# Row-maximum scores of two heads in separate halves of the partitions, and softmax denominators passed on by transfers, in a causal attention

## The chip, the cores and the metric

One Trainium2 chip, one core. The time is device time in microseconds of one execution of the whole program, the median of the runs; the profile is of one further execution.

## The reference

Two pre-norm layers on `x` of shape (4, 1024, 128), each an attention and a mixture of experts with residuals. The change touches the first attention only:

```python
def _L0_attn_ref(x, Wq, bq, Wk, bk, Wv, bv, Wo, bo):     # 16 heads of 8
    q, k, v = split_heads(x @ Wq + bq), split_heads(x @ Wk + bk), split_heads(x @ Wv + bv)
    scores = jnp.einsum('bhqd,bhkd->bhqk', q, k) / jnp.sqrt(8)
    scores = jnp.where(causal, scores, -10000.0)
    probs = jax.nn.softmax(scores, axis=-1)
    ctx = jnp.einsum('bhqk,bhkd->bhqd', probs, v)
    return ctx.transpose(0, 2, 1, 3).reshape(B, S, 128) @ Wo + bo
...
x = x + _L0_attn_ref(_layernorm(x, axis=-1), ...)
```

## The kernel before

`project` writes q and k to DRAM as three bf16 parts each (`q_parts`, `k_parts`). `attention0` walks 16 iterations `it`, each of one batch element and G = 4 heads, in 48 slots `p`. A product of q and k is the sum of the nine products of parts, so the operands `qs` and `ks` hold 9 x 8 = 72 partitions (STACK) for a head, and there are two kinds of scores.

- Scores for the maximum: queries on the partitions, `S`, a ring of three PSUM banks. The list `A` has 48 pieces for one iteration: query blocks 7 to 0, up to 512 keys each, four heads for each piece. PE multiplies, DVE reduces a piece to its maximum (`mx`). These run ahead (`AHEAD`, 72 slots): slots 0 to 23 of `it` make pieces 24 to 47 of iteration `it+1`, slots 24 to 47 pieces 0 to 23 of `it+2`. So the operands of `it+2` must be there at slot 24. They lie in one of three thirds of `qs` and `ks` (`half`).
- Transposed scores for the exponent: keys on the partitions, `ST`, two banks. Three further rows, STACK to STACK+2, hold minus the maximum in three parts against rows of ones, so the product comes out with the maximum subtracted. PE makes one piece a slot (`GROUPS`), ACT applies `Exp` into `eT`.

Every fourth slot PE multiplies `eT` of four heads by `vx` into `O`, four heads in four strips of 32 PSUM columns; row 8 of each strip gets the sum of the exponents. DVE copies `O` to `num` at slots 20 (`COPY0`, first half of the queries) and 4 of the next iteration (`COPY1`). PE multiplies `num` by `den_row`, which puts each head's sum on the rows of its strip (`extra`), DVE takes the reciprocal in eight pieces of 64 columns, one a slot from `RDEN0` = 36 and `RDEN1` = 10, and POOL multiplies (`normalize`) into `ctxT`.

The maximum: when `mx` is complete DVE makes `top` at slot 24, PE turns it to 32 x 128 in `extra` at slot 26, DVE splits it in `parts` (slots 27 to 30), and SP copies the three parts to the rows of `qs` (`store_max`).

SP issues all transfers, in the order of `step(it)`: `load(it+2)` (18) once the scores of slot 0 are made, `load_v(it+1)`, `store_max(it+1)` (3), `pack(it-1)` (4, to `packed`). PE waits for `max_in` at slot 0 and for `kq_in` before the first piece of an iteration. PE and DVE run a loop over iterations 1 to 13 with register offsets; the rest is written out. SP is written out in full.

Of the kernel before, what the change touches and what calls it, by code (L numbers as in the profile page):

```python
# [6 lines left out]
ALU = mybir.AluOpType  # L7
ACT = mybir.ActivationFunctionType
AX = mybir.AxisListType.X
# [5 lines left out]
P = 128  # L15
# [58 lines left out]
def build(nc, inp, out):  # L74
    k = Core()
    with ExitStack() as ctx:
        def sb(name, shape, dt=F32):
# [6 lines left out]
                    nc.dram_tensor("v_ones", (TOK, H * (HD + 1)), F32, kind="Internal").ap()]  # L84
        k.route_w = nc.dram_tensor("route_w", (B, 2), F32, kind="Internal").ap()
# [403 lines left out]
def attention0(nc, k, ctxT, packed):  # L489
# [18 lines left out]
    with ExitStack() as ctx:  # L508
# [3 lines left out]
        def sb(name, shape, dt=F32):  # L512
# [15 lines left out]
        score_s, max_s, top_s, turn_s, part_s = sem("score"), sem("max"), sem("top"), sem("turn"), sem("part")  # L528
        sturn_s, e_done, pv, oc, den_s, rden_s, ctx_s, vx_s = (
            sem(x) for x in ("sturn", "exp", "pv", "o_copied", "den", "rden", "ctx", "vx"))  # L530
# [42 lines left out]
        COPY0, DEN0, RDEN0 = G * FIRST_HALF + 4, G * FIRST_HALF + 18, G * FIRST_HALF + 20  # L573
        COPY1, DEN1, RDEN1 = 4, 8, 10
        RSTEPS = 8

        @block.sync
        def _(sp):
            def load(x):
                for u in range(SPLIT):  # L580
                    for y in range(SPLIT):
                        rows = slice((u * SPLIT + y) * HD, (u * SPLIT + y + 1) * HD)
                        for dst, src, s in ((qs, k.q_parts, u), (ks, k.k_parts, y)):
                            sp.dma_start(dst[rows, bass.ds(half(x), G * SEQ)].rearrange("d (g t) -> d g t", g=G),
                                         src[s, bass.ds(x * G * HD, G * HD), :].rearrange("(g d) t -> d g t", d=HD)).then_inc(kq_in, 16)
# [32 lines left out]

            sp.wait_ge(kones_s, 1)
            load(0)  # L620
            load_v(0)
            sp.wait_ge(kq_in, 16 * 2 * TERMS)
            load(1)
            store_max(0)
            for it in range(ITERS):
                step(it)
            pack(ITERS - 1)
            sp.wait_ge(packed_s, 16 * G * ITERS)
            sp.wait_ge(max_in, 16 * SPLIT * ITERS)
# [3 lines left out]
        def _(pe):  # L633
            def slot(it, p):
                x, r, na = max_piece(it, p)
                if x is not None:
                    i, j, lo, hi = A[r]
# [10 lines left out]
                if live(it):  # L648
                    hf, kb, lo, hi = GROUPS[p // G]
                    j = p % G  # L650
                    if p == 0:
                        pe.wait_ge(max_in, 16 * SPLIT * (it + 1))
# [1377 lines left out]
```

## Time and profile before

| | us |
|---|---|
| median of 3 runs | 4088.49 (4086.24 to 4089.66) |
| profiled execution, own time | 4076.11 |
| its span | 4074.2 |
| first attention, first issue of its loads to the product after it | 116.6 to 833.6 |
| DVE, PE, ACT busy in the whole span | 2963.6, 2823.3, 2477.3 |

Busy times are from records of single instructions; those of PE overlap, so a busy PE is not PE at its peak. PEclk is the granted clock of PE, 1.00 for 2.4 GHz and 0.50 for 1.2 GHz. An `x3` behind a row says that three like it were merged. In brackets stands how long the engine had been idle, and what released it.

### The profile page before, as it was taken

What the parts mean: (1) busy time and instruction counts of PE and PEld (TensorE: products, weight loads), DVE (VectorE), ACT (ScalarE), POOL (GpSimd) and SP (SyncE); (2) the same over time, 40 slices, a digit from 0 to 9 for tenths busy, and PEclk for the clock granted to TensorE, in tenths of its full rate; (3) what the DMA queues carried; (4) which work ended last, traced back from release to release, by engine and by line L of the source; (5) the groups of instructions that cost most, each with busy time, mean ns of one, the idle gap of its engine ahead of it and who ended that gap; (6) DMA issues with size and microseconds to landing.
All of it is one profiled execution on the core that took longest, in us unless ns stands there. A gap on an engine that the chain in (4) does not pass through costs nothing. (4 is left out here: it accounts for less than half of the span.)

```text
span 4074.2 us, 92993 instructions
## 1 busy us (share of the span) xinstructions
PE 2823.3 (69%) x25270; PEld 1692.7 (42%) x25318; DVE 2963.6 (73%) x10992; ACT 2477.3 (61%) x4212; POOL 1793.1 (44%) x4286
## 2 busy tenths in 40 slices
PE   3688888849554666656565666666666666665999
PEld 2133333336342444434343444444444444444665
DVE  6677777531454888888787888888888888864444
ACT  2155555624312888867686887888888888862222
POOL 3000000020013777756575776777776767653000
PEclk9699999959765666766666776776776776676999
DMA  3222232100012000001000001000001000000000
GB/s 111 39 36 35 33 39 30 19 8 26 10 50 72 5 4 7 4 4 36 4 4 4 7 4 36 4 7 4 4 13 27 7 4 5 6 1 27 6 8 8
DMA packets 131770, 77.04 MB, mean 19 GB/s; under 512 B 73287, under 2 KB 116055, under 8 KB 131463
## 3 DMA queue, kind: packets, MB, share of 16 engines
q1 hardware_dynamic: 131463, 74.32, 9.5%
q14 instruction: 282, 2.31, 0.2%
q8 instruction: 25, 0.41, 0.0%
HBM read 52.15 MB, written 19.14 MB: 17 GB/s over the span
## 5 line engine op out<-in xcount | busy, mean ns | idle before, releaser
L1130 PE MATMUL a_ST<-a_qs,a_ks 75*128 (+1 forms) x4096 | 732.0, 267 | 555.0 <-ACT a_eT L1174 540.0
L1230 POOL TENSOR_TENSOR a_near<-a_side,a_z 128x1024 int32<-128x1024 int32 x512 | 968.4, 1891 | 47.9 <-POOL a_side L1226 10.3
L1130 PEld LDWEIGHTS a_ST<-a_qs,a_ks 75*128 75x128 bf16 x4096 | 507.2, 125 | 709.8 <-issue 697.0
L1152 ACT ACTIVATE a_signs<-a_z,a_tiny 128x1024 bf16<-128x1024 f32 x512 | 588.3, 1149 | 218.0 <-DVE a_z L1348 203.3
L1348 DVE TENSOR_SCALAR_CACHE_REDUCE a_z<-a_S,a_thr 128x1024 f32<-128x1024 f32 x512 | 650.2, 1270 | 75.8 <-issue 53.8
L1145 ACT ACTIVATE a_signs<-a_S,search 128x1024 bf16<-128x1024 f32 x512 | 569.0, 1111 | 36.4 <-PE a_S L1079 36.4
L706 ACT ACTIVATE a_eT<-a_ST 128x512 f32<-128x512 f32 (+3 forms) x768 | 359.8, 490 | 363.4 <-PE a_ST L659 264.5
L1079 PE MATMUL a_S<-a_ks,a_qs 72*128 72x512 bf16 x1024 | 429.1, 512 | 214.0 <-DVE a_z L1348 163.8
L1174 ACT ACTIVATE a_eT<-a_ST 128x1024 f32<-128x1024 f32 x512 | 518.4, 1013 | 57.8 <-PE a_ST L1131 56.6
L1131 PE MATMUL a_ST<-ident_b,a_mask 128*128 128x128 bf16 x3072 | 505.7, 254 | 0.0
L773 DVE TENSOR_REDUCE a_mx<-a_S 128x1 f32<-128x512 f32 (+3 forms) x768 | 387.8, 535 | 158.2 <-PE a_S L643 110.7
L1095 PE MATMUL a_O<-a_eT,a_v 128*9 128x128 f32 x8192 | 376.3, 327 | 1.4 <-ACT a_oT L1180 1.4
L1131 PEld LDWEIGHTS a_ST<-ident_b,a_mask 128*128 128x128 bf16 x3072 | 358.6, 117 | 6.4
L643 PE MATMUL a_S<-a_ks,a_qs 72*128 (+4 forms) x768 | 271.4, 358 | 109.3 <-DMA a_ks<-k_parts 73.3
L1341 DVE TENSOR_SCALAR a_mask<-a_z,a_cut 128x1024 bf16<-128x1024 f32 x384 | 288.0, 750 | 56.4 <-issue 55.6
L1095 PEld LDWEIGHTS a_O<-a_eT,a_v 128*9 128x9 f32 x8192 | 212.8, 103 | 248.3 <-issue 217.4
L724 POOL TENSOR_TENSOR ctxT<-a_num,a_rden 128x512 f32 (+1 forms) x32 | 40.6, 1268 | 601.4 <-DVE a_rden L805 601.4
L656 PE MATMUL a_ST<-a_qs,a_ks 128*128 (+4 forms) x720 | 237.6, 333 | 18.6 <-ACT a_eT L706 13.1
L1167 ACT ACTIVATE a_mask<-a_z,a_cut_steep 128x1024 bf16<-128x1024 f32 x128 | 147.0, 1148 | 164.9 <-issue 132.7
L1131 PE MATMUL a_ST<-a_minus_b,a_mask 128*128 128x128 bf16 x1024 | 231.1, 313 | 0.0
L1386 DVE MAX8 a_cand<-a_near 128x8 f32<-128x256 f32 x512 | 213.6, 417 | 0.0
L1807 ACT ACTIVATE f_gate<-f_G 128x512 f32<-128x512 f32 x112 | 66.8, 597 | 239.2 <-PE f_W L1781 190.9
(331 smaller groups left out, 5837.2 us busy)
## 6 DMA issues: line engine op xcount, KB each, us to landing
a_ks<-k_parts SPq DMA_DIRECT2D x288, 64.0 KB
a_qs<-q_parts SPq DMA_DIRECT2D x144, 64.0 KB
a_qs<-q_parts SPq DMA_DIRECT2D x288, 32.0 KB
a_qs<-a_flip SPq DMA_DIRECT2D x512, 0.8 KB
q_parts<-p_qp SPq DMA_DIRECT2D x48, 128.0 KB, 1.7
k_parts<-p_kp SPq DMA_DIRECT2D x48, 128.0 KB, 1.8
f_w<-L_ffn_W SPq DMA_DIRECT2D x16, 256.0 KB, 2.5
v_ones<-p_vst SPq DMA_DIRECT2D x8, 288.0 KB, 2.4
```

The source lines that it names most:

```text
L706: act.activation(eT[:, gi % 4, p % G, 0:hi - lo], ST[p % 2][:, 0:hi - lo], ACT.Exp, scale=SCALE0).then_inc(e_done, 1)
L773: dve.tensor_reduce(mx[:, lo // CW, j * IB + i:j * IB + i + 1], S[r % 3][:, 0:hi - lo], AX, ALU.max).then_inc(max_s, 1)
L1079: mm = pe.matmul(S[h % 2][:, lo:lo + CW], qa, ks[0:STACK, h * SEQ + lo:h * SEQ + lo + CW], start=True, stop=True)
L1095: mm = pe.matmul(O[32 * j:32 * j + HD + 1, :], v[:, kb, head], eT[:, h0 % RING + j, kb * P:(kb + 1) * P], start=(kb == 0), stop=(kb == IB ...
L1130: pe.matmul(ST[:, block_of], ks[:, hl * SEQ + kb * P:hl * SEQ + (kb + 1) * P], qa, start=True, stop=False)
L1131: mm = pe.matmul(ST[:, block_of], mask[:, hl % MASKS, block_of], minus_b[:, :] if hl % 4 == 0 else k.ident_b[:, :], start=False, stop=True)
L1145: act.activation(signs[:, h % 2, :], S[h % 2][:, :], ACT.Sign, bias=first[:, bass.ds(n, 1)], accum_out=sgn[0][:, one]).then_inc(cnt1, 1)
L1152: act.activation(signs[:, 2, :], z[:, hl % RING, :], ACT.Sign, bias=tiny[:, :], accum_out=sgn[1][:, hl:hl + 1]).then_inc(cnt2, 1)
L1174: act.activation(eT[:, hl % RING, :], ST[:, :], ACT.Exp, scale=SCALE1).then_inc(e_done, 1)
L1230: pool.tensor_tensor(near[:, hl % 2, :].bitcast(I32), side[:, one].bitcast(I32).broadcast_to([P, SEQ]), z[:, hl % RING, :].bitcast(I32), A ...
L1341: dve.tensor_scalar(mask[:, hp % MASKS, :], z[:, hp % RING, :], cut[:, onep], AWAY, ALU.is_lt, ALU.mult).then_inc(mask_s, 1)
L1348: dve.tensor_scalar(z[:, h1 % RING, :], S[h1 % 2][:, :], thr1[:, one1], None, ALU.add, ALU.max, accum_out=zmax[:, one1]).then_inc(z_s, 1)
```

## The change

The nine terms of an even head lie in partitions 0 to 63 and, the ninth, 64 to 71; those of an odd head in 64 to 127 and 0 to 7. The scores for the maximum contract over 64 partitions, thus over eight of the nine terms, and are made for two heads in a row on even slots, each from its own half; `S` has a bank for each of the four heads, `extra` is gone. `load` issues 36 transfers of half the size. The maxima are split while the queries are on the partitions, four 32 x 32 block transposes turn them (`flip`), and `store_max` issues 16 transfers. The denominators: `gather` moves row 8 of each strip of `num` to `den16`, 32 partitions by 16 (four transfers), DVE takes one reciprocal of 128 x 16 at slot 34 or 18, `spread` stores it to DRAM, waits, and loads it to the eight rows of each strip (one and four). `step` has these in a new order. PE's instructions are written out with fixed addresses.

```diff
         mx, top = sb("mx", [P, 2, G * IB]), sb("top", [P, G * IB])
-        parts, left = sb("parts", [G * IB, SPLIT, P], BF16), sb("left", [G * IB, P])
+        parts, flip, left = sb("parts", [P, G, 32], BF16), sb("flip", [P, G, 32], BF16), sb("left", [P, G * IB])
+        den16, rec16 = sb("den16", [P, 2, 16]), sb("rec16", [P, 2, 16])
         eT = sb("eT", [P, 4, G, CW])
         num, rden = sb("num", [P, 2, CW]), sb("rden", [P, 2, CW])
-        S = [ctx.enter_context(nc.psum_tensor(f"a0_S{i}", [P, CW], F32)) for i in range(3)]
+        S = [ctx.enter_context(nc.psum_tensor(f"a0_S{i}", [P, CW], F32)) for i in range(4)]
...
-        extra = ctx.enter_context(nc.psum_tensor("a0_extra", [P, CW], F32))
...
         TOPAT, TURNAT = NA // 2, NA // 2 + 2
         PV_LAG = G + 2
-        COPY0, DEN0, RDEN0 = G * FIRST_HALF + 4, G * FIRST_HALF + 18, G * FIRST_HALF + 20
-        COPY1, DEN1, RDEN1 = 4, 8, 10
-        RSTEPS = 8
+        COPY0, RDEN0 = G * FIRST_HALF + 4, G * FIRST_HALF + 18
+        COPY1, RDEN1 = 4, 18
+        DMAS_Q, DMAS_MAX, DMAS_REC = 2 * 2 * TERMS, 4 * G, G + 1
+        PARTS = 5
 
         @block.sync
         def _(sp):
             def load(x):
+
                 for u in range(SPLIT):
                     for y in range(SPLIT):
-                        rows = slice((u * SPLIT + y) * HD, (u * SPLIT + y + 1) * HD)
-                        for dst, src, s in ((qs, k.q_parts, u), (ks, k.k_parts, y)):
-                            sp.dma_start(dst[rows, bass.ds(half(x), G * SEQ)].rearrange("d (g t) -> d g t", g=G),
-                                         src[s, bass.ds(x * G * HD, G * HD), :].rearrange("(g d) t -> d g t", d=HD)).then_inc(kq_in, 16)
+                        t = u * SPLIT + y
+                        for odd in range(2):
+                            at = (t * HD + 64 * odd) % P if t < 8 else 64 * (1 - odd)
+                            for dst, src, part in ((qs, k.q_parts, u), (ks, k.k_parts, y)):
+                                sp.dma_start(dst[at:at + HD, bass.ds(half(x), G * SEQ)].rearrange("d (a e t) -> d a e t", a=G // 2, e=2)[:, :, odd, :],
+                                             src[part, bass.ds(x * G * HD, G * HD), :].rearrange("(a e d) t -> e d a t", a=G // 2, e=2)[odd]).then_inc(kq_in, 16)
...
             def store_max(x):
-                sp.wait_ge(part_s, 4 * x + 4)
-                for s in range(SPLIT):
-                    sp.dma_start(qs[STACK + s:STACK + s + 1, bass.ds(half(x), G * SEQ)].rearrange("o (c q) -> o c q", q=P),
-                                 parts[:, s, :]).then_inc(max_in, 16)
-
-            def step(it):
-                more = not (isinstance(it, int) and it + 2 >= ITERS)
-                if more:
-
-
-                    sp.wait_ge(score_s, NA * it + (AHEAD + 1))
-                    load(it + 2)
-                if not (isinstance(it, int) and it + 1 >= ITERS):
-                    sp.wait_ge(vx_s, 2 * it + 1)
-                    load_v(it + 1)
-                    store_max(it + 1)
-                if it > 0:
-                    pack(it - 1)
+                sp.wait_ge(flip_s, x + 1)
+                for j in range(G):
+                    at = STACK if j % 2 == 0 else HD
+                    rows = qs[at:at + SPLIT, bass.ds(half(x) + j * SEQ, SEQ)].rearrange("s (i g r) -> s i g r", i=IB, g=4)
+                    for g in range(4):
+                        sp.dma_start(rows[:, :, g, :], flip[32 * g:32 * g + SPLIT * IB, j, :]).then_inc(max_in, 16)
+
+            def gather(x, hf):
+
+                sp.wait_ge(oc, 2 * x + hf + 1)
+                for j in range(G):
+                    sp.dma_start(den16[32 * j:32 * j + 32, hf, :],
+                                 num[32 * j + HD:32 * j + HD + 1, hf, :].rearrange("o (b c) -> o b c", c=16)).then_inc(den_in, 16)
+
+            def spread(x, hf):
+
+                sp.wait_ge(rec_s, 2 * x + hf + 1)
+                sp.wait_ge(ctx_s, 2 * x + hf + 1)
+                sp.dma_start(k.den_rows[hf].rearrange("j (b c) -> (j b) c", c=16), rec16[:, hf, :]).then_inc(rden_in, 16)
+                sp.wait_ge(rden_in, 16 * (DMAS_REC * (2 * x + hf) + 1))
+                for j in range(G):
+                    sp.dma_start(rden[32 * j:32 * j + HD, hf, :], k.den_rows[hf, j:j + 1, :].broadcast_to([HD, CW])).then_inc(rden_in, 16)
...
+            def step(it):
+                if it + 2 < ITERS:
+                    sp.wait_ge(score_s, NA * it + (AHEAD + 2))
+                    load(it + 2)
+                if it > 0:
+                    gather(it - 1, 1)
+                if it + 1 < ITERS:
+                    sp.wait_ge(vx_s, 2 * it + 1)
+                    load_v(it + 1)
+                if it > 0:
+                    spread(it - 1, 1)
+                gather(it, 0)
+                if it > 0:
+                    pack(it - 1)
+                if it + 1 < ITERS:
+                    store_max(it + 1)
+                spread(it, 0)
+
             sp.wait_ge(kones_s, 1)
             load(0)
             load_v(0)
-            sp.wait_ge(kq_in, 16 * 2 * TERMS)
+            sp.wait_ge(kq_in, 16 * DMAS_Q)
             load(1)
             store_max(0)
             for it in range(ITERS):
                 step(it)
+            gather(ITERS - 1, 1)
...
+                if x is not None and p % 2 == 0:
+                    i, j0, lo, hi = A[r]
                     if r == 0:
-                        pe.wait_ge(kq_in, 16 * 2 * TERMS * (x + 1))
-                    if not (it is None and na < 3):
+                        pe.wait_ge(kq_in, 16 * DMAS_Q * (x + 1))
+                    if not (it is None and na < 4):
                         pe.wait_ge(max_s, na - 2)
                     diag = hi == (i + 1) * P
-                    mm = pe.matmul(S[r % 3][:, 0:hi - lo], qs[0:STACK, bass.ds(half(x) + j * SEQ + i * P, P)],
-                                   ks[0:STACK, bass.ds(half(x) + j * SEQ + lo, hi - lo)], start=True, stop=not diag)
+                    for j in (j0, j0 + 1):
+                        rows = slice(64 * (j % 2), 64 * (j % 2) + 64)
+                        mm = pe.matmul(S[j][:, 0:hi - lo], qs[rows, half(x) + j * SEQ + i * P:half(x) + j * SEQ + (i + 1) * P],
+                                       ks[rows, half(x) + j * SEQ + lo:half(x) + j * SEQ + hi], start=True, stop=not diag)
+                        if not diag:
+                            mm.then_inc(score_s, 1)
                     if diag:
-                        mm = pe.matmul(S[r % 3][:, hi - lo - P:hi - lo], k.ident_b[:, :], k.causal_b[:, :], start=False, stop=True)
-                    mm.then_inc(score_s, 1)
+                        for j in (j0, j0 + 1):
+                            pe.matmul(S[j][:, hi - lo - P:hi - lo], k.ident_b[:, :], k.causal_b[:, :],
+                                      start=False, stop=True).then_inc(score_s, 1)
...
-                if p == DEN1 and live(before(it)):
-                    pe.wait_ge(oc, 2 * it)
-                    pe.wait_ge(rden_s, 2 * it - 1)
-                    pe.matmul(extra[:, :], k.den_row[:, :], num[:, 1, :], start=True, stop=True).then_inc(den_s, 1)
-                x = topped(it, p, TURNAT)
-                if x is not None:
-                    pe.wait_ge(top_s, x + 1)
-                    if not (isinstance(x, int) and x < 2):
-                        pe.wait_ge(rden_s, 2 * x - 2)
-                    elif x == 1:
-                        pe.wait_ge(part_s, 4 * x)
-                    pe.transpose(extra[0:G * IB, 0:P], top[:, :], k.ident[:, :]).then_inc(turn_s, 1)
-                if p == DEN0 and live(it):
-                    pe.wait_ge(oc, 2 * it + 1)
-                    if isinstance(it, int) and it + 1 >= ITERS:
-                        pe.wait_ge(rden_s, 2 * it)
-                    else:
-                        pe.wait_ge(part_s, 4 * it + 6)
-                    pe.matmul(extra[:, :], k.den_row[:, :], num[:, 0, :], start=True, stop=True).then_inc(den_s, 1)
-            run(slot, pe)
+            for it, ps in [(None, range(-AHEAD, 0))] + [(it, range(NB_)) for it in range(ITERS)] + [(ITERS, range(NB_ // 2))]:
+                for p in ps:
+                    slot(it, p)
...
 
             def normalize(x, hf):
-                pool.wait_ge(rden_s, 2 * x + hf + 1)
+                pool.wait_ge(rden_in, 16 * DMAS_REC * (2 * x + hf + 1))
                 pool.tensor_tensor(ctxT[:, bass.ds(x, 1), hf * CW:(hf + 1) * CW].rearrange("p o t -> p (o t)"),
                                    num[:, hf, :], rden[:, hf, :], ALU.mult).then_inc(ctx_s, 1)
...
-            pool.nop().then_inc(ctx_s, 1)
+            pool.memset(rden[:, :, :], 1.0).then_inc(ctx_s, 1)
...
         def _(dve):
 
 
-            dve.memset(qs[64:P, :], 0.0)
-            dve.memset(ks[64:P, :], 1.0)
+            for rows, odd in ((slice(64, P), 0), (slice(0, 64), 1)):
+                by_head = lambda a: a[rows, :].rearrange("d (a e t) -> d a e t", e=2, t=SEQ)[:, :, odd, :]
+                dve.memset(by_head(qs), 0.0)
+                dve.memset(by_head(ks), 1.0)
+            dve.memset(parts[:, :, :], 0.0)
             dve.memset(mx[:, 1, :], GONE).then_inc(kones_s, 1)
+            dve.wait_ge(kones_s, 1)
...
-                    dve.tensor_tensor(top[:, :], mx[:, 0, :], mx[:, 1, :], ALU.max).then_inc(top_s, 1)
+                        dve.wait_ge(part_s, PARTS * x)
+                    dve.tensor_tensor(top[:, :], mx[:, 0, :], mx[:, 1, :], ALU.max).then_inc(part_s, 1)
...
+                        dve.wait_ge(part_s, PARTS * x - (PARTS - 1))
+                    dve.tensor_reduce(mx[:, lo // CW, j * IB + i:j * IB + i + 1], S[j][:, 0:hi - lo], AX, ALU.max).then_inc(max_s, 1)
+                part = lambda u: parts[:, :, u * IB:(u + 1) * IB]
+                by_head = lambda a: a[:, :].rearrange("p (j i) -> p j i", i=IB)
+                x = topped(it, p, TURNAT)
+                if x is not None:
...
+                    dve.tensor_scalar(part(0), by_head(top), -1.0, None, ALU.mult).then_inc(part_s, 1)
...
                 if x is not None:
-                    dve.wait_ge(part_s, 4 * x + 3)
-                    dve.tensor_tensor(parts[:, 2, :], left[:, :], parts[:, 1, :], ALU.subtract).then_inc(part_s, 1)
+                    dve.wait_ge(part_s, PARTS * x + 5)
+                    if not (isinstance(x, int) and x == 0):
+                        dve.wait_ge(max_in, 16 * DMAS_MAX * x)
+                    for j in range(G):
+                        ins = dve.transpose(flip[:, j, :], parts[:, j, :])
+                    ins.then_inc(flip_s, 1)
...
                 for at, hf, y in ((RDEN1, 1, before(it)), (RDEN0, 0, it)):
-                    if at <= p < at + RSTEPS and live(y):
-                        if p == at:
-                            dve.wait_ge(den_s, 2 * y + hf + 1)
-                        cols = slice((p - at) * CW // RSTEPS, (p - at + 1) * CW // RSTEPS)
-                        ins = dve.reciprocal(rden[:, hf, cols], extra[:, cols])
-                        if p == at + RSTEPS - 1:
-                            ins.then_inc(rden_s, 1)
+                    if p == at and live(y):
+                        dve.wait_ge(den_in, 16 * G * (2 * y + hf + 1))
+                        if not (isinstance(y, int) and y == 0):
+                            dve.wait_ge(rden_in, 16 * DMAS_REC * (2 * y + hf - 1))
+                        dve.reciprocal(rec16[:, hf, :], den16[:, hf, :]).then_inc(rec_s, 1)
```

## Rows read from the trace of the kernel before

**Rows 1.** Windows, by iterations: us, PE, PEld, DVE, ACT, POOL busy (x), PEclk, DMA share, GB/s
```profile
135.00:174.00 39.00, 36.87 (x120) 9.79 (x122) 37.17 (x78) 0.00 (x0) 0.52 (x2) 0.50 0.23 32
...
214.60:254.30 39.70, 35.33 (x258) 14.22 (x263) 32.13 (x72) 22.60 (x48) 3.29 (x5) 1.00 0.28 39
546.30:589.40 43.10, 36.67 (x259) 14.54 (x261) 32.19 (x71) 22.63 (x48) 3.07 (x5) 0.96 0.28 34
589.40:630.00 40.60, 36.38 (x259) 14.63 (x261) 32.25 (x71) 22.71 (x48) 3.06 (x4) 0.96 0.29 36
...
757.00:792.00 35.00, 29.90 (x224) 10.89 (x225) 18.82 (x47) 22.47 (x50) 3.06 (x4) 1.00 0.06 9
```

**Rows 2.** Timeline of SP's queue: start us, us, issue; parts of three iterations
```profile
164.93 1.90 SPq L594 DMA_DIRECT2D a_qs<-a_parts  x3
173.51 0.28 SPq L584 DMA_DIRECT2D a_qs<-q_parts  x1
...
546.37 0.28 SPq L584 DMA_DIRECT2D a_qs<-q_parts  x1
...
552.20 0.30 SPq L584 DMA_DIRECT2D a_ks<-k_parts  x1
552.54 0.39 SPq L588 DMA_DIRECT2D a_vst<-v_rows  x1
574.90 1.83 SPq L594 DMA_DIRECT2D a_qs<-a_parts  x3
576.77 2.73 SPq L616 DMA_DIRECT2D packed<-ctxT  x4
589.46 0.28 SPq L584 DMA_DIRECT2D a_qs<-q_parts  x1
...
715.64 0.28 SPq L584 DMA_DIRECT2D a_qs<-q_parts  x1
```

**Rows 3.** Timeline of PE, rows released by the load: first, tenth and last of 14
```profile
193.17 0.43 PE L643 MATMUL a_S<-a_ks,a_qs 72*128 72x512 bf16 x1 [3.47 <-DMA a_ks<-k_parts]
...
567.12 0.39 PE L643 MATMUL a_S<-a_ks,a_qs 72*128 x1 [2.74 <-DMA a_ks<-k_parts]
...
736.18 0.39 PE L643 MATMUL a_S<-a_ks,a_qs 72*128 x1 [1.30 <-DMA a_ks<-k_parts]
```

**Rows 4.** Timeline of DVE (first four) and PE, spacing of neighbouring operations
```profile
136.30 16.36 DVE L773 TENSOR_REDUCE a_mx<-a_S 128x1 f32<-128x512 f32 x32 [19.72 <-PE a_S L643]
...
152.90 6.68 DVE L773 TENSOR_REDUCE a_mx<-a_S 128x1 f32<-128x512 f32 x16 [0.24 <-PE a_S L646]
...
557.00 0.54 DVE L805 RECIPROCAL a_rden<-a_extra 128x64 f32<-128x64 f32 x1
...
557.87 0.54 DVE L805 RECIPROCAL a_rden<-a_extra 128x64 f32<-128x64 f32 x1
...
480.60 1.06 PE L673 MATMUL a_O<-a_eT,a_vx 128*32 128x512 f32 x8
...
484.87 0.38 PE L656 MATMUL a_ST<-a_qs,a_ks 128*128 x1
485.09 0.38 PE L643 MATMUL a_S<-a_ks,a_qs 72*128 x1
```

**Rows 5.** Groups by line and shape, 50 to 832 us
```profile
L724 POOL TENSOR_TENSOR ctxT<-a_num,a_rden 128x512 f32 x28 | 35.5, 1268 | 492.9 <-DVE a_rden L805 492.9
...
L694 PE MATMUL a_extra<-a_num,den_row 128*128 128x512 f32 x32 | 18.0, 645 | 0.0
L679 PE MATMUL a_extra<-a_num,den_row 128*128 128x512 f32 x32 | 17.3, 621 | 0.8 <-DVE a_num L799 0.8
...
L766 DVE TENSOR_TENSOR a_top<-a_mx 128x32 f32<-128x32 f32 x16 | 3.1, 192 | 0.5
```

**Rows 6.** One line's issues (ns min/median/max) and landings: L1021, L588, L594, L481
```profile
L1021 SPq DMA_DIRECT2D a_qs<-a_flip x512: 697/698/763, 1311.5 to 3637.1; - x171
L1402 DVE STREAM_TRANSPOSE a_flip<-a_parts x128: 181/192/197, 1311.3 to 3634.6; 128x32 bf16<-128x32 bf16 x128
...
DMA to landing us min/median/max: 2.5/13.7/15.2
...
DMA to landing us min/median/max: 1.8/1.9/3.2
...
DMA to landing us min/median/max: 1.7/1.7/1.8
```

**Rows 7.** Windows while a load runs and after it, columns as in rows 1
```profile
598.00:602.00 4.00, 3.99 (x41) 1.77 (x40) 3.98 (x8) 1.93 (x6) 0.00 (x0) 1.00 0.53 66
...
609.00:612.00 3.00, 2.56 (x14) 0.73 (x14) 1.89 (x3) 1.95 (x4) 0.00 (x0) 1.00 0.00 0
```

**Rows 8.** Windows before the scores of iteration 0, columns as in rows 1
```profile
88.00:135.00 47.00, 0.46 (x5) 0.27 (x3) 19.09 (x9) 3.27 (x5) 4.81 (x5) 0.53 0.33 64
```

More of the change, by code:

```diff
@@ L84, in build @@
                     nc.dram_tensor("v_ones", (TOK, H * (HD + 1)), F32, kind="Internal").ap()]
+        k.den_rows = nc.dram_tensor("den_rows", (2, 4, CW), F32, kind="Internal").ap()
         k.route_w = nc.dram_tensor("route_w", (B, 2), F32, kind="Internal").ap()
@@ L626, in _ @@
                 step(it)
+            gather(ITERS - 1, 1)
+            spread(ITERS - 1, 1)
             pack(ITERS - 1)
             sp.wait_ge(packed_s, 16 * G * ITERS)
-            sp.wait_ge(max_in, 16 * SPLIT * ITERS)
+            sp.wait_ge(max_in, 16 * DMAS_MAX * ITERS)
             sp.wait_ge(v_in, 16 * ITERS)
@@ L651, in slot @@
                     if p == 0:
-                        pe.wait_ge(max_in, 16 * SPLIT * (it + 1))
+                        pe.wait_ge(max_in, 16 * DMAS_MAX * (it + 1))
                     if not (isinstance(it, int) and it == 0 and p < 2):
@@ L655, in slot @@
                     diag = lo == kb * P
-                    mm = pe.matmul(ST[p % 2][:, 0:hi - lo], ks[:, bass.ds(half(it) + j * SEQ + kb * P, P)],
-                                   qs[:, bass.ds(half(it) + j * SEQ + lo, hi - lo)], start=True, stop=not diag)
+                    mm = pe.matmul(ST[p % 2][:, 0:hi - lo], ks[:, half(it) + j * SEQ + kb * P:half(it) + j * SEQ + (kb + 1) * P],
+                                   qs[:, half(it) + j * SEQ + lo:half(it) + j * SEQ + hi], start=True, stop=not diag)
                     if diag:
@@ L776, in slot @@
                 if x is not None:
-                    dve.wait_ge(turn_s, x + 1)
-                    if not (isinstance(x, int) and x == 0):
-                        dve.wait_ge(max_in, 16 * SPLIT * x)
-                    dve.tensor_scalar(parts[:, 0, :], turned, -1.0, None, ALU.mult).then_inc(part_s, 1)
+                    dve.wait_ge(part_s, PARTS * x + 2)
+                    dve.scalar_tensor_tensor(by_head(left), by_head(top), -1.0, part(0), ALU.mult, ALU.subtract).then_inc(part_s, 1)
@@ L782, in slot @@
                 x = topped(it, p, TURNAT + 2)
                 if x is not None:
-                    dve.wait_ge(part_s, 4 * x + 1)
-                    dve.scalar_tensor_tensor(left[:, :], turned, -1.0, parts[:, 0, :], ALU.mult, ALU.subtract).then_inc(part_s, 1)
+                    dve.wait_ge(part_s, PARTS * x + 3)
+                    dve.tensor_copy(part(1), by_head(left)).then_inc(part_s, 1)
                 x = topped(it, p, TURNAT + 3)
                 if x is not None:
-                    dve.wait_ge(part_s, 4 * x + 2)
@@ L789, in slot @@
-                    dve.tensor_copy(parts[:, 1, :], left[:, :]).then_inc(part_s, 1)
+                    dve.wait_ge(part_s, PARTS * x + 4)
+                    dve.tensor_tensor(part(2), by_head(left), part(1), ALU.subtract).then_inc(part_s, 1)
                 x = topped(it, p, TURNAT + 4)
                 if x is not None:
-                    dve.wait_ge(part_s, 4 * x + 3)
-                    dve.tensor_tensor(parts[:, 2, :], left[:, :], parts[:, 1, :], ALU.subtract).then_inc(part_s, 1)
+                    dve.wait_ge(part_s, PARTS * x + 5)
@@ L794, in slot @@
+                    if not (isinstance(x, int) and x == 0):
+                        dve.wait_ge(max_in, 16 * DMAS_MAX * x)
+                    for j in range(G):
+                        ins = dve.transpose(flip[:, j, :], parts[:, j, :])
+                    ins.then_inc(flip_s, 1)
                 for at, hf, y in ((COPY1, 1, before(it)), (COPY0, 0, it)):
```

14 lines of the change are left out of this document (5 added, 9 removed).

## The prediction

> **What bounds the kernel now.** I read first the windows cut at the steps of the first attention [rows 1]: iterations of about 41 us, with PE busy 36.4 us (its records overlap), DVE 32.3 and ACT 22.7 of some 40.6. No engine is full, so a wait must set part of the pace. The order of SP's issues [rows 2] gives the frame: iteration `it` starts when SP issues the load of `it+2` (slot 0 of its 48), at 173.51 for the first and 715.64 for the fourteenth: 13 intervals, 41.7 us on average. The PE rows that waited for the load [rows 3] give the first half: in all 14 iterations with a load, PE stands at slot 24 (the first scores of `it+2`) until the load has landed, 193.17 - 173.51 = 19.7 us, 567.12 - 546.37 = 20.8 us and 736.18 - 715.64 = 20.5 us after its first issue. So the first 24 slots are bound by the load, about 20.3 us. The second half, 567.12 to 589.46, is 22 us; there DVE is the fullest engine: of 48 reduces in 16.36 + 6.68 = 23.0 us back to back [rows 4], the 24 of the second half (16 of 512 columns) are some 13 us; with eight reciprocals of 0.45 us (a reciprocal and a reduce of 384 columns repeat every 0.87 us, the reduce alone takes about 0.42) and the parts it has about 18.
>
> **What the change takes off the engines.** DVE: 16 reciprocals an iteration, 16 x 0.45 = 7.2 us, become two on 128x16, priced as the 128x32 `top` at 0.19 us each [rows 5]. The four part operations on 32x128 (0.20 to 0.27 us) turn into ones on 128x32 (about 0.19), and four transposes at 0.19 are new. DVE goes from 32 to about 25 us. PE: two 512-column f32 products with `den_row` (two records each, of 0.62 and 0.65 us [rows 5], about 1 us together) and one transpose go: 2.3 us. The 48 score products of one iteration have 18,432 columns; neighbouring 512-column products start 0.22 us apart [rows 4], so 7.9 us; if the two halves of the partitions run at once, 3.9 are left, if not, 7.9. PE's second half is then 9,216 columns for the transposed scores (4.0), 10,752 for the scores of two heads at a time (2.3), 28 diagonals at 0.06 (1.7), and six groups of products with `vx`, 1.0 for four of them [rows 4] and 1.4 for the two shorter (5.4): 13.4 us, and the first half somewhat less. ACT keeps 22.7. So if engines alone decided, an iteration could come down towards 30 us. PE's straight-line code replaces a loop; the straight iteration 757 to 792 [rows 1] shows no loss from that, and I price it at nothing: PE is not what ends last below. PSUM stays at eight banks.
>
> **What it adds to SP, in SP's order.** The prices per issue: loads follow one another every 0.343 us ((552.20 - 546.37)/17) [rows 2]; three `parts` rows take 1.82 us, four `packed` copies 2.73 us, so a transfer from SBUF to SBUF costs 0.61 to 0.68. The same kind as the new `flip` copies exists in the second attention, 512 of them, never below 0.697 us [rows 6]; with the gap behind it I take 0.73. Landing: 1.9 us for a small one, 1.7 for a store to DRAM [rows 6].
> Let the first load issue be 0.
> - Load: 36 issues instead of 18, 36 x 0.343 = 12.4.
> - `gather(it-1,1)`: four from one partition to 32, at 0.68 (bounds 0.61 and 0.73): 15.1. Then `load_v`: 15.5.
> - `spread(it-1,1)` waits for DVE's reciprocal at slot 18, this for `den_in`, and the gather was issued behind the load on the same queue. What such a transfer meets is shown by `vst` in the kernel before: issued behind the load, it lands after 13.7 us in the median, where 2.5 us is the least [rows 6], that is 20 us after the load's first issue, together with the load.
> - When does the new load land? While it ran, the share of the 16 DMA engines is 0.53 and the rate 66 GB/s [rows 7]; 18 x 64 KB at that rate are 18 us. Transfers with eight partitions thus keep about eight engines busy. The new ones are 36 x 32 KB, eight partitions again, the same runs of 2 KB. I take the same time and 0.9 us more for 18 further completions: landed at 21.0, `den_in` at 21.5. Bounds: at the rate of issue, 12.4 + 1.9 = 14.3 (then the gather's own landing decides, its last issue at 14.4 + 1.9 = 16.3, `den_in` 16.7); and, if half-size transfers cost a third more, 26.5.
> - Reciprocal and hand-over: 21.8. The store to `den_rows` lands at 23.7, SP standing there; four broadcasts at 0.34: 25.1, the last lands at 26.7.
> - `gather(it,0)`: 27.8 (slot 20's copy is done by then). POOL's product, 1.27 us [rows 5], ends at 28.0, and only then `pack`: 30.7.
> - `store_max(it+1)`: `flip` is made at slot 30, about 5 us after slot 24 resumes at 23.5, so it is ready. 16 x 0.73 = 11.7: 42.4. The last lands at 43.6, and PE's slot 0 of the next iteration waits for it.
> - `spread(it,0)`: 1.9 + 1.4: 45.7. Only now can the next load be issued. With the semaphore hops, 46.0.
>
> The engines' second half, 24 slots at DVE's 14 to 16 us, ends at about 39 and is hidden under `store_max`; so is the first half, 11 us of DVE and 12 of ACT, under the load. The gain on DVE and PE is real and lands in waits. The period is `den_in` + 24.5, and SP alone now issues for 36 us of it.
>
> The Trainium skill, "DMA: Bandwidth & Descriptors", section "Why a DMA increments its semaphore by 16 and not by 1", says that a transfer uses the largest number of engines up to 16 that divides the slowest dimension of both sides, the lowest-numbered ones. That gives eight for the old and the new load, and 16 for `vst` and the gather, so part of the gather lies behind the load. The share of 0.53 agrees; that half-size loads behave so, no row shows. By the page alone the bound of 14.3 is out and the period is 46.
>
> **The sum.** Iterations 1 to 13: 13 x (46.0 - 41.7) = +55.9. Iteration 0 has no `gather(-1,1)`, spread or pack: about 41, as before. Start: 16 `flip` copies instead of three parts rows before slot 0. The parts were ready at 164.93 and slot 0 came at 173.51 [rows 2]; now SP is busy to 165.4 + 11.7 = 177.1: +4. The new memsets cover as many elements as the old. End: iterations 14 and 15 hold no load; 757 to 834 now; with fewer reciprocals and no stall at slot 24 about 3 us less each in DVE work, but a tail of gather, store, broadcast, product and pack of 17 us against 12: together -3. Sum +57 us. The profiled execution took 4076.1 us (its span 4074.2), 0.3% under the median of 4088.5; the difference is carried to the median: 4145.
>
> **Rivals.**
> *The load lands as fast as it is issued* (other side). With 32 KB pieces on more engines, `den_in` comes at 16.7, the period is 16.7 + 24.5 = 41.2, iteration 0 is some 4 us shorter: 13 x (-0.5) - 4 + 4 - 3 = -9.5, so 4079. It decides from `den_in` under 17.2 us. For it: the rate of issue would allow 14.3. Against: the shape stays at eight partitions and [rows 7] at half of the engines. 10%; another 6% that `den_in` comes near 17.5 and nothing changes.
> *The clock.* Between its last free score bank (slot 20 or so) and the landing PE now stands some 12 us. In this trace the clock was granted at 1.00 in steady iterations and 0.96 in those with a wait of nearly 3 us; from 135 to 174, after 40 us with PE idle, it stayed at 0.50, the level of 1.2 GHz, all through PE's weaker work [rows 1, 8]. If the second half ran wholly at 0.50, PE's 13.4 us there would be 26.8, slot 0 would come at 23.5 + 26.8 = 50.3, later than SP: 13 x 8.6 + 1 = +113, 4201. For it: the long wait in each iteration. Against: PE is full when it resumes, and the first 5 us are covered by SP. 17%.
> The Trainium skill, "TensorE: Matmul & The Clock Gate", section "Loop structure matters more than you think", names a long DMA wait in a loop as what makes matmuls run cold. That is this rival, and the page would favour 4201 over 4145.
> *Half-size loads cost more each.* Landed at 26.5, period 51.5: 13 x 9.8 + 1 = +128, 4217. 8%.
> *PE's halves don't run at once:* PE has 4 us more a period, all hidden: 4145 still, part of the likeliest case.
>
> **Chances.** Likeliest case 59%, the clock 17%, the load early 10%, near no change 6%, costly halves 8%. The likeliest has a range of its own, 4120 to 4165, from a microsecond or two a period in the issue prices. With the clock's case and the space around both, 4100 to 4202 holds eight in ten. Two kernels within 0.2% (8 us) can't be told apart here. Faster: 0.10; same: 0.06; slower: 0.84.
>
> **What would show it.** In the profile after: iterations of 46 us; the chain of SP's issues without a gap from `pack` through 16 `flip` copies to the next load; DVE waiting at slot 18 for `den_in` until about 21.5 us after the load's first issue; PE waiting for `flip` copies at slot 0; DVE busy 25 us an iteration. The prediction is wrong if the load lands before 17 us, if `flip` copies issue well below 0.7 us, or if the iterations' length follows the granted clock.

## The result, and the profile of the changed kernel

| | before | after |
|---|---|---|
| median (6 runs each) | 4088.23 | 4102.78 |
| profiled execution: span | 4074.2 | 4101.2 |
| start to first load of the first attention | 116.6 | 118.0 |
| first attention, first load to output product | 717.1 | 762.7 |
| from there to the second attention | 457.3 | 459.7 |
| second attention, first to last score product | 2330.2 | 2308.4 |
| rest | 453.0 | 452.4 |

The changed kernel takes 1.0043 times as long, 95% interval 1.0029 to 1.0057: 15 to 18 us slower, where 57 were predicted. The profiled executions differ by 27 us, 12 more than the medians, because that of before lay 12 us under its median.

The table holds two things: the first attention lost 46 us, and the second, in which the diff changes nothing, gave 22 back.

**The first attention.** Windows of iterations 1 and 7 (of 0 to 15), columns as in rows 1:

```profile
220.30:263.30 43.00, 36.55 (x264) 11.63 (x256) 26.40 (x62) 22.27 (x49) 3.00 (x4) 0.88 0.22 39
486.50:531.50 45.00, 35.62 (x256) 11.43 (x248) 26.28 (x63) 22.16 (x48) 3.00 (x4) 0.88 0.27 37
```

DVE is down from 32.2 [rows 1] to 26.3 us, ACT unchanged, and the iteration is longer: the work came off, and waits took its place. SP's queue in that iteration (its load begins at 486.55; of its 36 rows only the first is shown), and the waits of over 1.3 us that DVE and PE have in it:

```profile
486.55 0.30 SPq L589 DMA_DIRECT2D a_qs<-q_parts  x1
...
499.76 2.48 SPq L608 DMA_DIRECT2D a_den<-a_num  x4
502.29 0.59 SPq L593 DMA_DIRECT2D a_vst<-v_rows  x1
506.85 0.36 SPq L615 DMA_DIRECT2D den_rows<-a_rec  x1
508.30 1.30 SPq L618 DMA_DIRECT2D a_rden<-den_rows  x4
509.64 2.42 SPq L608 DMA_DIRECT2D a_den<-a_num  x4
512.37 2.74 SPq L625 DMA_DIRECT2D packed<-ctxT  x4
516.69 11.94 SPq L602 DMA_DIRECT2D a_qs<-a_flip  x16
528.73 0.36 SPq L615 DMA_DIRECT2D den_rows<-a_rec  x1
530.17 1.29 SPq L618 DMA_DIRECT2D a_rden<-den_rows  x4
```

```profile
491.80 6.01 DVE L794 TENSOR_REDUCE a_mx<-a_S 128x1 f32<-128x512 f32 x11 [1.85 <-PE a_S L680]
506.57 0.25 DVE L834 RECIPROCAL a_rec<-a_den 128x16 f32<-128x16 f32 x1 [8.76 <-DMA a_den<-a_num]
511.02 1.89 DVE L794 TENSOR_REDUCE a_mx<-a_S 128x1 f32<-128x512 f32 x3 [2.21 <-PE a_S L674]
```

```profile
507.16 0.29 PE L674 MATMUL a_S<-a_ks,a_qs 64*128 64x128 bf16 x2 [7.49 <-DVE a_mx L794]
529.71 0.39 PE L690 MATMUL a_ST<-a_qs,a_ks 128*128 128x512 bf16 x1 [1.43 <-DMA a_qs<-a_flip]
```

Read them in order of time. SP issues the load for 13 us and the gather behind it. DVE stands 8.8 us at slot 18 until the gather has landed, 20.0 us after the load's first issue (17.0 to 20.5 in iterations 1 to 12, 19.1 on average). PE runs out of score banks and stands 7.5 us behind DVE. Then SP stores, waits, broadcasts, gathers and packs; behind that only one gap is left, 515.11 to 516.69, in which it waits for `flip`. Sixteen copies, a store and four broadcasts later, at 531.5, comes the next load. It is SP's own issues, the landing behind the load and this wait of 1.6 us that make the period.

**The second attention.** What DVE waited for between its first and last score product, three of the lines: total us, times, longest. L1384 of before and L1411 of after are one instruction, the first after DVE has read a flag and branched on it:

```profile
DVE a_rest L1384 <- issue: 118.8, 126, 4.4
DVE a_mask L1341 <- issue: 54.5, 129, 0.6
DVE a_z L1348 <- issue: 53.8, 25, 4.7
```

```profile
DVE a_rest L1411 <- issue: 100.0, 126, 4.4
DVE a_z L1375 <- issue: 64.9, 30, 4.9
DVE a_mask L1368 <- issue: 48.1, 129, 0.6
```

Busy times are the same within 0.5% (DVE 2004.8 and 2002.2 us). The idle times before `a_rest` and `a_mask`, which wait for nothing that the profile shows, fell by 19 and 6 us; the one before `a_z` rose by 11, and smaller waits for POOL and PE moved both ways. All of DVE's idle time together fell by 19 us.

### The profile page after: what moved, and what is told of

Read it like the earlier page. It is cut to its first block and busy times, and to the rows that moved or that the text cites. A ratio compares the mean times of both kernels' runs of the same rounds, so it can differ in the third digit from the quotient of the medians.

```text
span 4101.2 us, 91264 instructions
## 1 busy us (share of the span) xinstructions
PE 2790.2 (68%) x25238; PEld 1639.8 (40%) x25238; DVE 2867.9 (70%) x10835; ACT 2470.2 (60%) x4212; POOL 1792.6 (44%) x4287
## 5 line engine op out<-in xcount | busy, mean ns | idle before, releaser
L690 PE MATMUL a_ST<-a_qs,a_ks 128*128 128x512 bf16 (+3 forms) x768 | 262.4, 359 | 42.3 <-DMA a_qs<-a_flip 26.9
L674 PE MATMUL a_S<-a_ks,a_qs 64*128 64x512 bf16 (+3 forms) x768 | 141.3, 365 | 150.6 <-DVE a_mx L794 98.1
```

## Experiments

A ratio is to the kernel before on the same chip. The kernel before took 4077.1 us on the chip of e5, e6, e8 and e9, 4089.7 on that of e1 to e4 and 4102.6 on that of e10 and e11, and ratios from different chips do not agree as closely as their intervals: e1 and e8, of one price as it turns out, have 1.0094 and 1.0146. So across chips I compare stages. "First" and "second" are the lengths of the two attentions in the profile, as in the table. The first attention varies between kernels in which its code is the same: it took 717.1, 717.7 and 711.9 us in three of the old form and 762.7, 759.8 and 751.5 in three of the new, so the median loss is 43 us.

### DVE's instructions ahead of the second attention: e1, e2

The programs have 768 (before) and 744 (after) DVE instructions ahead of the first that works on the second attention's scores. Both kernels get more, on DVE, behind the first attention's output product, 24 in the changed kernel (e1) and 40 in the kernel before (e2):

```diff
                 dve.tensor_tensor(x, y_ps[n % 4][:, :, :], x, ALU.add).then_inc(x_s, 1)
+            for _ in range(24):
+                dve.nop().then_inc(x_s, 1)
```

> The kernel after, with 24 semaphore increments by DVE behind its last addition of the first output product, so that DVE's code of the second attention stands where it stood in the kernel before (768 instructions in front of it instead of 744). The computation is unchanged. In the profiles the second attention, from its first to its last score product, took 2330.1 us before and 2308.4 after, though none of its instructions is changed. Theory A (where DVE's instructions lie sets the price of its branches): back to 2330, whole 4125. Theory B (where PE's instructions lie, 2354 more in front of them now): stays at 2308, whole 4104. Theory C (the time at which the stage starts, by way of the clock): the start moves by 1 us only, so about 2308.

> The kernel before, with 40 such increments by DVE at the same place: 808 instructions in front of the second attention, which is 24 fewer than 768 if only the place within a block of 64 (or 32, 16) counts. The computation is unchanged. Theory A: the second attention takes 2308 instead of 2330, whole about 4067. Theories B and C: 2330, whole 4089.

Measured: e1 ratio 1.0094 (1.0067 to 1.0120), second 2334.2. e2 ratio 0.9944 (0.9925 to 0.9962), second 2315.5. Adding 24 increments made the changed kernel 21 us slower by the ratios, 25 by the medians; adding 40 made the kernel before 23 us faster, of which the stage shows 15. The wait before the same instruction in e1:

```profile
DVE a_rest L1413 <- issue: 118.7, 126, 4.4
```

and in e2:

```profile
DVE a_rest L1386 <- issue: 99.7, 126, 3.9
```

The second attention began at 1291.0 in before, 1294.8 in e2, 1340.4 in the changed kernel and 1341.9 in e1: dear, cheap, cheap, dear, so its start time is not the cause.

### PE written out in the kernel before: e3

```diff
-            run(slot, pe)
+            for it, ps in [(None, range(-AHEAD, 0))] + [(it, range(NB_)) for it in range(ITERS)] + [(ITERS, range(NB_ // 2))]:
+                for p in ps:
+                    slot(it, p)
```

> One part of the change alone: the kernel before with PE's instructions of the first attention written out with fixed addresses instead of a loop; 3874 PE instructions in front of the second attention instead of 1425. The computation is unchanged. First attention (716 us from the first to the last of its loads' issue to the output product) within 5 us of before. Theory B: the second attention changes by 10 us or more. Theories A and C: it stays at 2330, whole 4084 to 4090.

Measured: ratio 0.9990 (0.9975 to 1.0005), first 725.3, second 2332.1. The place of PE's instructions does nothing to the second attention. The first attention missed its 5 us: it took 8 us more, within the 11 us by which kernels with the same code for it differ above. The whole shows no loss, so nothing here speaks against pricing the straight code at nothing; that the stage loses nothing is not shown.

### How wide the dear place is: e8, e9

e1 with 88 increments instead of 24 (832 DVE instructions ahead); e2 with 8 instead of 40 (776).

> The changed kernel with 88 semaphore increments on DVE behind the first output product, 64 more than in e1, so DVE has 832 instructions ahead of the second attention. They cost at most 88 x 0.07 us = 6 us themselves. Theory (the place of DVE's instructions against some grid of 64 instructions or a divisor of it sets the price of its branches in the second attention): the second attention takes about 2332 us, as in e1 with 768 instructions, and the whole about 4130. Rival (the price depends on the position otherwise, for instance it is high in one place only): second attention 2308 to 2316, the whole about 4107.

> The kernel before with 8 semaphore increments on DVE behind the first output product: 776 instructions ahead of the second attention, where the kernel before has 768 and e2 had 808. Theory of a grid of 64 instructions with a low price over part of it: somewhere between 2310 and 2332 us for the second attention; if 8 instructions are enough to leave the dear place, the second attention is near 2312 us and the whole near 4068; if the dear place is wider than 8 instructions, 2330 us and 4088.

Measured: e8 ratio 1.0146 (1.0128 to 1.0164), second 2338.3. e9 ratio 1.0022 (1.0012 to 1.0032), second 2339.0, above the 2310 to 2332 that were expected. So 64 instructions more than in e1 leave the price where it was, and 8 more than in before are not enough to leave the dear place.

### The maxima by way of DRAM: e4

The sixteen `flip` copies become four stores to a DRAM buffer, in the order of the rows, and two loads for all four heads:

```diff
-                for j in range(G):
-                    at = STACK if j % 2 == 0 else HD
-                    rows = qs[at:at + SPLIT, bass.ds(half(x) + j * SEQ, SEQ)].rearrange("s (i g r) -> s i g r", i=IB, g=4)
-                    for g in range(4):
-                        sp.dma_start(rows[:, :, g, :], flip[32 * g:32 * g + SPLIT * IB, j, :]).then_inc(max_in, 16)
+                if x > 1:
+                    sp.wait_ge(max_in, 16 * DMAS_MAX * (x - 1))
+                turned = k.max_rows[x % 2].rearrange("j c (g r) -> c j g r", g=4)
+                for g in range(4):
+                    sp.dma_start(turned[:, :, g, :], flip[32 * g:32 * g + SPLIT * IB, :, :]).then_inc(max_in, 16)
+                sp.wait_ge(max_in, 16 * (DMAS_MAX * x + 4))
+                flat = k.max_rows[x % 2].rearrange("(a e) (s i) q -> e s a (i q)", e=2, s=SPLIT)
+                for odd in range(2):
+                    at = STACK if odd == 0 else HD
+                    rows = qs[at:at + SPLIT, bass.ds(half(x), G * SEQ)].rearrange("s (a e q) -> s a e q", a=G // 2, e=2)
+                    sp.dma_start(rows[:, :, odd, :], flat[odd]).then_inc(max_in, 16)
```

> The kernel after, but the maxima go from flip to DRAM in four transfers and from there to their rows in two, instead of 16 from SBUF to SBUF. The computation is unchanged. Theory S (SP's chain sets the pace): store_max takes 3.8 us instead of 12, the next load is issued as soon as slot 0 is reached, so an iteration falls from 44.6 to the 41.3 us that the engines' waits leave; first attention 43 us shorter, whole 4060. Rival (the engines' own waits at den_in and the slower second half set the pace): iterations stay at 44 to 45 us, whole 4095 to 4103.

Measured: ratio 0.9903 (0.9877 to 0.9929), first 711.8, second 2307.9, the period 41.7, as the first of the two readings had it. SP's queue in one iteration of e4:

```profile
532.23 2.72 SPq L632 DMA_DIRECT2D packed<-ctxT  x4
537.41 1.56 SPq L603 DMA_DIRECT2D max_rows<-a_flip  x4
539.99 0.55 SPq L609 DMA_DIRECT2D a_qs<-max_rows  x2
540.64 0.35 SPq L622 DMA_DIRECT2D den_rows<-a_rec  x1
```

The step takes 3.1 us instead of 12.0, yet the next load comes only some 3 us sooner: SP now waits 2.5 us, 534.95 to 537.41, for `flip`, because DVE still loses its 8 us at slot 18:

```profile
526.34 0.25 DVE L841 RECIPROCAL a_rec<-a_den 128x16 f32<-128x16 f32 x1 [7.99 <-DMA a_den<-a_num]
```

With SP's chain shortened, that wait is what counts next.

### The reciprocal at slot 23: e5, e10

`RDEN1` goes from 18 to 23, in e4 (e5) and in the changed kernel (e10).

```diff
-        COPY1, RDEN1 = 4, 18
+        COPY1, RDEN1 = 4, 23
```

> The kernel with the maxima passed by DRAM (e4), with the second reciprocal of an iteration moved from slot 18 to slot 23, the last slot that the closing part of the last iteration still runs. In e4 DVE stood 8.0 us at slot 18 for the gathered denominators and all reduces of slots 18 to 23 came behind it. Theory (DVE's wait at slot 18 holds the first half's engines back by the work of five slots, about 3 us): those reduces are done while the gather is under way, the 24 slots after it start with less in arrears, and the period of the first attention goes from 41.6 to 38 or 39 us; the first attention takes about 670 us, the whole 4005 to 4015. Rival (SP alone sets the period: the gather's landing, store, broadcasts, product, packed copies and the six transfers of the maxima follow whatever DVE does meanwhile): period 41 to 41.6, the whole 4040 to 4050. Second attention as in e4, 2308.

> The changed kernel with the second reciprocal of an iteration moved from slot 18 to slot 23, the sixteen flip copies kept. In the changed kernel SP stands from the last packed copy until DVE has made the transposed maxima: 1.5 to 1.6 us an iteration, since DVE comes late out of its wait at slot 18. Theory (the chain of the changed kernel is den_in, then DVE's and PE's slots up to 30, then 16 flip copies of 0.73 us, then the spread): the flips are ready when the packed copies have been issued, the period goes from 44.6 by 1.0 to 1.8 us down, to 43 or 43.5, the first attention takes 740 to 750 us, the whole 4077 to 4092. Rival (five slots of DVE's work, about 3 us, come off each iteration as in e4 to e5, which gave 4.2 us a period): the whole 4050 to 4060. Rival (nothing): 4103.

Measured: e5 ratio 0.9803 (0.9785 to 0.9820), first 653.4, second 2309.8, period 37.1. e10 ratio 0.9974 (0.9961 to 0.9986), first 750.0, second 2313.0, period 43.3. The one edit is worth 58 us in the first attention with the maxima by DRAM, and 10 us in the changed kernel (759.8, the median of three, to 750.0), where the sixteen copies lie behind it; e10's ratio lies below the changed kernel's by more than that, but on a chip on which before took 4102.6 us and not 4088.2, so I read the stage. e10's period was forecast; e5 gained more than forecast (period 38 to 39, first 670). SP in e10:

```profile
506.26 2.74 SPq L625 DMA_DIRECT2D packed<-ctxT  x4
509.05 11.94 SPq L602 DMA_DIRECT2D a_qs<-a_flip  x16
521.09 0.36 SPq L615 DMA_DIRECT2D den_rows<-a_rec  x1
```

There is no gap left before the copies: what e10 gained is the wait for `flip`. What remains is the landing, 20.0 us in this iteration, and SP's chain behind it. In e5 SP's queue in the second half is

```profile
465.29 1.66 SPq L603 DMA_DIRECT2D max_rows<-a_flip  x4
467.96 0.55 SPq L609 DMA_DIRECT2D a_qs<-max_rows  x2
468.62 0.35 SPq L622 DMA_DIRECT2D den_rows<-a_rec  x1
470.13 1.29 SPq L625 DMA_DIRECT2D a_rden<-den_rows  x4
475.09 0.28 SPq L590 DMA_DIRECT2D a_qs<-q_parts  x1
```

so SP is done 3.7 us before the engines reach the slot at which the next load may go, and PE is again released by the load, as in the kernel before [rows 3], 18.4 us after the load's first issue at 437.28 (16.1 to 19.5 in 13 iterations, 18.4 the median):

```profile
455.70 0.39 PE L681 MATMUL a_S<-a_ks,a_qs 64*128 64x512 bf16 x2 [2.77 <-DMA a_ks<-k_parts]
```

### The gather as one transfer: e6, and its other place: e11

```diff
-                for j in range(G):
-                    sp.dma_start(den16[32 * j:32 * j + 32, hf, :],
-                                 num[32 * j + HD:32 * j + HD + 1, hf, :].rearrange("o (b c) -> o b c", c=16)).then_inc(den_in, 16)
+                sp.dma_start(den16[:, hf, :], num[HD:P:32, hf, :].rearrange("j (b c) -> j b c", c=16)).then_inc(den_in, 16)
```

DVE's wait is changed to match, for 16 and not 64. e11 is e6 with 16 increments on DVE, as in e1: 760 instructions ahead.

> e5 with each gather issued as one transfer (four partitions to 128) in place of four. If SP's issues set the period, each of the two gathers of an iteration gives back three issues of 0.61 us, 1.8 us: the one behind the load lets the denominators arrive up to 1.8 us earlier, the one for the first half lies on SP's chain itself; the period is 2 to 3.5 us under e5's and the whole 30 to 50 us under it. If the landing of the load and of what is queued behind it sets the first half, only the second gather counts, at most 1.8 us a period, 25 us. If the engines set it, it is that of e5.

> e6 (maxima by DRAM, late reciprocal, gather as one transfer) with 16 semaphore increments on DVE behind the first output product: 760 instructions ahead of the second attention, 56 past a multiple of 64. Seen so far: 2330 to 2339 us for the second attention at 768, 776 and 832 (0, 8 and 0 past a multiple of 64), 2308 to 2316 at 744 and 808 (40 past it). If the price follows the distance to the last multiple of 64 and the cheap part is around 40, the second attention takes 2305 to 2320 us and the whole 3988 to 4003; if the dear part begins before the multiple, 2330 and 4013. At 40, e6 took 3991.

Measured: e6 ratio 0.9795 (0.9779 to 0.9811), first 653.5, second 2309.1: as e5. Fewer issues on a queue that no longer sets the pace are worth nothing that these runs could measure, the third of the readings written down. e11 ratio 0.9792 (0.9761 to 0.9823), first 662.3, second 2328.2. The ratio is as low as e6's and by itself would say that the 16 increments cost nothing; the 20 us of the dear place would make it 0.984. But it is of another chip, and e11's four executions (4010.7, 4012.5, 4025.5, 4025.8, the last one profiled) lie further apart than most. What decides is the wait in the profile:

```profile
DVE a_rest L1418 <- issue: 118.8, 126, 4.4
```

where e5, 16 instructions shorter, has

```profile
DVE a_rest L1418 <- issue: 99.9, 126, 4.4
```

and e10, on e11's own chip, with 744 instructions,

```profile
DVE a_rest L1411 <- issue: 99.8, 126, 4.4
```

So e11's wait is the dear one, against the first of its two readings; in the whole time it is not shown.

## Why the prediction was wrong

The sign was right, and so was the mechanism in the first attention. The size was wrong: 4103 lies below the likeliest case (4120 to 4165), in which e1, without the gain in the second attention, lies at 4128. That it is just inside 4100 to 4202 is luck: no case of the prediction had that gain. Between the profiled executions the first attention gave +45.6 where the sum had +57 (a period predicted at 46.0 us and measured at 44.6 is the largest part of that), the second -21.8 where it had nothing, and the rest +3.2 (+1.4 before the first load, +2.4 between the attentions, -0.6 behind the second): +27. The other 12 us down to the medians' +15 are the profiled execution of before, which was fast by its own median; the prediction had carried its difference over that gap, but a single execution is known no better than that.

**The step that failed: the sum took in only the first attention.** It put everything behind the stage at nothing, and gave no reason. The second attention's instructions stayed as they were, but not its time: 2330.2 to 2308.4 us. e1 puts the 24 DVE instructions back that the change had taken away, and the gain of 22 us is gone: ratio 1.0094, which on 4088 is +38 us, still under the +57. In order of instructions ahead of the second attention, counted past the last multiple of 64:

| kernel | ahead | past 64 | wait before `a_rest` | second |
|---|---|---|---|---|
| before | 768 | 0 | 118.8 | 2330.2 |
| e1 | 768 | 0 | 118.7 | 2334.2 |
| e8 | 832 | 0 | 118.8 | 2338.3 |
| e9 | 776 | 8 | 116.8 | 2339.0 |
| after | 744 | 40 | 100.0 | 2308.4 |
| e5 | 744 | 40 | 99.9 | 2309.8 |
| e10 | 744 | 40 | 99.8 | 2313.0 |
| e2 | 808 | 40 | 99.7 | 2315.5 |
| e11 | 760 | 56 | 118.8 | 2328.2 |

That the number of DVE instructions ahead sets the price is shown, both ways, and each of the three chips of the experiments has shown both prices. It goes up and down with the number (744 cheap, 760 to 776 dear, 808 cheap, 832 dear), so it is no threshold. The other three agree: e3, with 768, waits 118.8, and e4 and e6, with 744, wait 99.9. A repeat every 64 instructions fits all nine kernels, and so does one every 128; that there is a repeat at all is read from six numbers and not shown further. A repeat every 32 does not: 744, 776 and 808 are all 8 past a multiple of 32, and 776 is dear. Why the instruction behind the branch waits longer in one place than in another was not measured and stays open, as do the 8 to 11 us by which kernels of one price differ among each other.

**The terms of the first attention.** From the load starts (173.51 and 715.64 in [rows 2] for before; 179.9, 220.3 and 756.0 after, for iterations 0, 1 and 13):

- *Start, +4.* Slot 0 of iteration 0 comes 61.9 us after the first load, 56.9 before: +5.0. Right.
- *Iteration 0, 0.* It takes 40.4 us, 41.1 before: -0.7.
- *Period, 46.0, the mis-sized term.* Iterations 1 to 12 take 44.6 on average, so 12 x (44.6 - 41.75) = +34.6, where 12 x 4.3 = 51.6 was predicted: 17 us, the largest error within the sum. `den_in` comes at 19.1 on average instead of 21.5. The chain from there to the next load is longer than 24.5: 44.6 - 19.1 = 25.5 on average, 24.9 in the iteration shown. There the store and the broadcasts take 3.0 (predicted 3.6, since the store landed in 1.45 and not 1.9), the gather 2.4 (2.7), the packed copies 2.7 as priced, then comes the wait of 1.6 for `flip`, which had been called ready (it was made 30.1 us after the load's first issue and not 28.5, and SP stood there at 28.6 and not 30.7), the copies take 11.9 (11.7) and the second spread 2.7 (3.3).
- *The load.* It was said to land at 21.0, bounds 14.3 and 26.5. In the changed kernel nothing waits for it alone. Where PE does, it lands at 18.4 in the median in e5 (16.1 to 19.5) and at 19.1 in e10 (17.0 to 20.1): twice as many transfers of half the size take nearly as long as the old ones (19.7 to 20.8 [rows 3]), neither as little as the issues allow nor a third more. So half-size loads do not cost more each, and the load does not land as fast as it is issued, though `den_in` came under that rival's 17.2 us in two of the twelve iterations. The rate of the old load [rows 7], 18 us for as many bytes, comes nearest; the 3 us put on top of it were too much.
- *End, -3.* Iteration 13 and the end together are +6.6, where the sum had 4.3 - 3 = +1.3. Iteration 14 has no load but still its sixteen copies; slot 0 of iteration 15 waits for them until 832.71, and from the last copy to `num`, 865.65, to the output product at 880.7 are 15.1 us, where the kernel before had 11.5. The sum had looked at DVE's work there, which sets nothing.

**The clock.** The rival at 4201 asked for PE's second half at 0.50 throughout. PE was granted 0.50 for some time after its long wait, and 0.88 over the iteration where it had been 0.96 to 1.00 [rows 1]:

```profile
504.00:510.00 6.00, 2.84 (x14) 0.55 (x14) 2.11 (x8) 0.60 (x1) 0.00 (x0) 0.50 0.23 24
```

That stretch lies ahead of SP's copies, and slot 0 was released by the `flip` copies, not by PE's own work. But DVE waits 2.2 us for PE there, 508.81 to 511.02, and then SP 1.6 us for `flip`; how much of that is the clock's was not measured. The rule of the Trainium skill, "TensorE: Matmul & The Clock Gate", section "Loop structure matters more than you think", names the long wait in a loop as what makes matmuls run cold, and the trace agrees that it did. What it did not do here is set the end of the iteration.

**The engines** were priced right: DVE predicted at 25 us an iteration, measured 26.3. The 6 us that the change takes off DVE bring nothing while SP sets the period. Once the maxima go by DRAM and the reciprocal lies at slot 23, the first attention is 64 us shorter than before (the second 20, by its 744 instructions ahead), and e5, at 0.98 of the time, is faster than both kernels. Of its 4.6 us a period (41.7 to 37.1) some 1.9 are the load, which lands at 18.4 us in the median of e5 and 20.3 in that of before; the rest is the second half, where the engines have less to do.

## What to carry to other kernels

Before work is moved from an engine to transfers, add up the issues on the queue that gets them: sixteen copies from SBUF to SBUF are 12 us of a queue's time, and what waits behind them matters more than what they replace. After the first bottleneck is taken away, look for the wait that hid behind it: one line separates e4 from e5, and it is worth 58 us of the stage.

A sum over the changed stage is a forecast of that stage. Compare each unchanged stage too before a small difference is put down to the edit, and where a later stage with branches has moved, change the number of instructions ahead of it and look again.

## What was not expected of the hardware

- The same DVE code, with the same data, took 2308 to 2316 or 2328 to 2339 us depending on how many DVE instructions stand ahead of it. The idle time before the instruction behind a branch is 0.79 us, or 0.93 to 0.94, in the mean of 126.
- The gather's landing hardly depends on how it is issued: behind the load, in four transfers, it released DVE 19.3 us after the load's first issue in the median of e5, in one transfer after 18.3 in e6, with the load itself at 18.4 and 18.5.
- Stores from SBUF to DRAM with the `flip` layout were issued in 0.38 us each in the median (L603 in e5), the copies of the same data from SBUF to SBUF in 0.70.
